# A cross-attention block in float32 on one core: the TensorE order goes from pairs of steps to fours

## What is computed

```python
x = layer_norm(hidden_states, ln1_w, ln1_b)
q = (x @ q_w + q_b)   # 8 x 256 x 256, split in 16 heads of 16
k = (encoder_hidden_states @ k_w + k_b)
v = (encoder_hidden_states @ v_w + v_b)
scores = jnp.einsum('bhqd,bhkd->bhqk', q, k) * scale
scores = jnp.where(mask, scores, mask_value)
attn = jax.nn.softmax(scores, axis=-1)
out = jnp.einsum('bhqk,bhkd->bhqd', attn, v)
out = out.transpose(0, 2, 1, 3).reshape(B, LQ, D) @ cproj_w + cproj_b
hidden = out + residual
y = layer_norm(hidden, ln2_w, ln2_b)
y = jax.nn.gelu(y @ fc_w + fc_b, approximate=True) @ proj_w + proj_b
return hidden + y
```

## Time and profile before

| | |
|---|---|
| median of 3 runs | 770.86 us (765.46 to 772.29) |
| profiled execution, device time | 768.76 us |
| its span (first to last instruction) | 767.0 us |
| TensorE (PE) busy | 702.5 us, 92% |
| ScalarE (ACT) busy | 446.1 us, 58% |
| VectorE (DVE) busy | 371.3 us, 48% |
| mean granted TensorE clock | 0.965 of full speed |

### The profile page before, as it was taken

How to read it: one execution, slowest core, us unless ns; L and a number is a source line. 1 busy time by engine, 2 the same in 40 slices (tenths; PEclk the granted TensorE clock), 3 DMA queues, 4 the chain that set the end, 5 groups by cost and what they waited for, 6 DMA issues and landing times.

```text
span 767.0 us, 16866 instructions
## 1 busy us (share of the span) xinstructions
PE 702.5 (92%) x7026; PEld 478.5 (62%) x7026; DVE 371.3 (48%) x824; ACT 446.1 (58%) x475; POOL 120.9 (16%) x90
## 2 busy tenths in 40 slices
PE   3657699899999999999999999999998978999997
PEld 3545466566656656666566566656664544597897
DVE  6643355265436534643464446534642331467663
ACT  3004366856676677567756775676566788733321
POOL 5222002200220032003201220131000600110010
PEclk9867799999999999999999999999999989999999
DMA  9787578657874788477938694878475800000000
GB/s 312 216 186 131 186 184 188 179 138 183 189 203 128 174 188 217 143 180 158 235 123 203 148 246 123 192 153 230 132 165 126 253 6 2 1 21 8 29 28 31
DMA packets 51275, 113.78 MB, mean 148 GB/s; under 512 B 7050, under 2 KB 40178, under 8 KB 49914
## 3 DMA queue, kind: packets, MB, share of 16 engines
q1 hardware_dynamic: 40700, 80.47, 44.5%
q10 hardware_dynamic: 10494, 32.17, 13.8%
HBM read 65.30 MB, written 47.06 MB: 146 GB/s over the span
## 4 chain that ended last, share of the span: by engine, by line
PE 76%; ACT 13%; DMA 5%; DVE 3%; issue 2%; ACTq 1%; DVEq 0%
PE O L1126 21%; PE S L1119 16%; ACT pr L583 11%; PE O L1056 10%; PE XB L1056 10%; PE O L1213 6%; PE S L1056 6%; DMA k_scr<-kpart 2%; DMA qst<-q_scr 2%; PE XB L1093 2%; PE XB L1153 2%; PE MB L1106 2%; DVE kpart L725 1%; DVE kpart L728 1%; DMA cols_s<-in_cols 1%
## 5 line engine op out<-in xcount | busy, mean ns | idle before, releaser
L583 ACT ACTIVATE pr<-S 128x1024 f32<-128x1024 f32 x416 | 400.6, 1024 | 188.6 <-PE S L1119 184.4
L1126 PE MATMUL O<-pr,vsl 128*17 128x256 f32 x3328 | 227.4, 388 | 1.3 <-DVE ot L790 1.3
L1119 PEld LDWEIGHTS S<-qst,kst 50*128 50x128 f32 x1664 | 117.1, 188 | 120.4 <-ACT pr L583 81.4
L1119 PE MATMUL S<-qst,kst 50*128 50x256 f32 x1664 | 171.7, 315 | 18.7 <-ACT pr L583 15.0
L1126 PEld LDWEIGHTS O<-pr,vsl 128*17 128x17 f32 x3328 | 75.3, 97 | 79.2 <-issue 17.7
L725 DVE TENSOR_SCALAR kpart<-O,cols_s 128x384 fp32r<-128x384 f32 x64 | 40.6, 635 | 120.7 <-PE O L1056 120.7
L771 DVE TENSOR_REDUCE mx<-MB 128x2 fp32r<-128x512 f32 x64 | 44.1, 690 | 79.0 <-PE MB L1106 79.0
L510 POOL CAST c_hi<-cT 128x768 fp32r<-128x768 f32 (+1 forms) x28 | 23.9, 852 | 348.0 <-DMA cT<-in_ctx_t 235.8
L1056 PE MATMUL XB<-w_hi,c_hi 128*128 128x256 f32 (+1 forms) x208 | 68.3, 328 | 2.1 <-DVE vsl L739 1.3
L739 DVE TENSOR_TENSOR vsl<-XB,rows_s 128x256 f32<-128x256 f32 (+1 forms) x104 | 43.3, 417 | 55.1 <-PE XB L1056 55.1
L1056 PE MATMUL O<-c_hi,w_hi 128*128 128x384 f32 (+1 forms) x128 | 52.6, 411 | 17.7 <-POOL c_lo L515 10.3
(11 more groups left out here) (100 smaller groups left out, 825.6 us busy)
## 6 DMA issues: line engine op xcount, KB each, us to landing
kst<-k_scr SPq DMA_DIRECT2D x59, 400.2 KB
k_scr<-kpart SPq DMA_DIRECT2D x48, 384.0 KB, 8.0
v_scr<-vsl ACTq DMA_DIRECT2D x8, 1768.0 KB, 11.9
kst<-k_scr SPq DMA_DIRECT2D x59, 200.1 KB
cT<-in_ctx_t ACTq DMA_DIRECT2D x21, 384.0 KB, 7.6
k_scr<-kpart SPq DMA_DIRECT2D x16, 449.0 KB, 7.1
q_scr<-qpart SPq DMA_DIRECT2D x16, 256.0 KB, 2.5
qst<-q_scr SPq DMA_DIRECT2D x59, 64.0 KB
```

The lines of the kernel that those rows point to most:

```text
L583: nc.scalar.activation(pr[:, n % PBUF, :], S[:, 2 * (n % 2):2 * (n % 2) + 2, :] .rearrange("p a n -> p (a n)"), ACT.Exp).then_inc(s_.exp_d ...
L1119: last = nc.tensor.matmul(S[:, 2 * (n % 2) + g_, j * LQ:(j + 1) * LQ], kst[rows_, s, j, kt * P:(kt + 1) * P], qst[rows_, s, j, :], start=T ...
L1126: last = nc.tensor.matmul(O[32 * h:32 * h + VW, 0, 0:LQ], vsl[:, par, s, kt, h * VW:(h + 1) * VW], pr[:, n % PBUF, h * LQ:(h + 1) * LQ], s ...
```

## The change

The tables now go by fours ("quads") of steps, 13 a batch. A four is: its max unit, the scores of two steps, its V, xt, q or cproj unit (`x_units`), its K unit, the scores of the other two steps, and then the value products of four steps, those numbered 4i-2 to 4i+1. One V unit now makes two key tiles (12 matmuls, one read-out of 512 columns), so there are 7 instead of 13. There is at most one K unit and one unit of `x_units` in a four: K units in fours 0, 1, 3, 4, 5, 7, 8 and 10, V units in 0, 5, 6, 9, 10, 11 and 12 (the last has one tile), cproj in 1, xt in 2, q in 3, max units in 1, 2, 5, 6, 8, 9, 11 and 12. In batch 7 only cproj, y's transposes (four 9) and the max units of fours 1, 2, 5 and 6 are left. STRADDLE is empty: where a slot ends inside a four (i = 3, after its third step; i = 10, after its first; i = 0 of the next batch, after its second), the next step's value products stand right behind, and wait for `o_taken`; VectorE has its read-outs of the four's units ahead of the `take_o`. The buffers `pr` go from 4 to 6, the encoder states and `vsl` change their layout, `max_evac` reads KB first, the head is put in another order, SyncE's list of stores and fills follows the new order, `store_v` always goes at n = 10, `load_mlp` moves from n = 44 of batch 6 to n = 4 of batch 7, and y's transposes of batch 7 go to n = 38. Numbers of matmuls, exponentials and transfers and their bytes stay.

The diff, cut to its core:

```diff
-PBUF = 4
+PBUF = 6
 STEPS = SLOTS * KT
-PAIRS = STEPS // 2
+QUADS = STEPS // 4
...
-K_AT = {0: (0, 0), 2: (0, 1), 4: (0, 2), 6: (0, 3), 8: (1, 0), 10: (1, 1), 12: (1, 2), 14: (1, 3)}
...
-CPROJ_AT, XT_AT, Q_AT = 3, 4, 5
...
-STRADDLE = (7, 20)
+K_AT = {0: (0, 0), 1: (0, 1), 3: (0, 2), 4: (0, 3), 5: (1, 0), 7: (1, 1), 8: (1, 2), 10: (1, 3)}
...
+CPROJ_AT, XT_AT, Q_AT = 1, 2, 3
+STRADDLE = {}
...
+KV = -(-KT // 2)
...
-        vsl = sb("vsl", [P, 2, SLOTS, KT, HG * VW], F32)
+        vsl = sb("vsl", [P, 2, KT, H * VW], F32)
...
                 first_fill(sp, b, 3)
                 if b + 1 < B:
-                    for c in range(3):
-                        store_k(b + 1, 0, c)
+                    store_k(b + 1, 0, 0)
+                    store_k(b + 1, 0, 1)
                 first_rows(b, 2)
                 if b + 1 < B:
+                    store_k(b + 1, 0, 2)
                     store_q(b + 1)
                     store_k(b + 1, 0, 3)
                     first_fill(sp, b + 1, 0)
                     store_k(b + 1, 1, 0)
-                    store_k(b + 1, 1, 1)
                 first_rows(b, 3)
                 if b + 1 < B:
+                    store_k(b + 1, 1, 1)
+                    first_fill(sp, b + 1, 1)
                     store_k(b + 1, 1, 2)
-                    first_fill(sp, b + 1, 1)
+                    first_rows(b + 1, 0)
                     store_k(b + 1, 1, 3)
-                    first_rows(b + 1, 0)
                     first_fill(sp, b + 1, 2)
                     first_rows(b + 1, 1)
...
             for b in range(B):
                 for n in range(STEPS):
-                    if n == 10 and b == 0:
-                        store_v(0)
+                    if n == 10:
+                        store_v(b)
                     if n in CTX_AT and b + 2 < B:
                         next_ctx(b + 2, CTX_AT.index(n))
-                    if n == 48 and b + 1 < B:
-                        store_v(b + 1)
-                    if n == 44 and b + 2 == B:
+                    if n == 4 and b + 1 == B:
                         load_mlp()
-                    if b == 0 and n == 40:
+                    if b == 0 and n == 46:
                         x_root(2 * QT, TOK, XB_VAR)
                     if b == B - 1 and n == 20:
                         h_root(first, 0, 0, HEAD)
-                    if b == B - 1 and n == 2 * YT_AT + 4:
+                    if b == B - 1 and n == 4 * YT_AT + 6:
                         act.wait_ge(mlpw_lo, 2)
                         y_t(first, 0)
-                    exponential(first, b, n)
+                    exponential(first, b, n, (STEPS * b + n) % PBUF)
...
-            def v_evac(b, kt):
-                m = TAIL if kt == KT - 1 else P
-                if kt == 0:
+            def v_evac(b, i):
+                tiles = slice(2 * i, min(2 * i + 2, KT))
+                m, n = (P, 2) if i < KV - 1 else (TAIL, 1)
+                if i == 0:
                     dve.wait_ge(pads_set, 7 if b == 0 else 10)
                     if b >= 2:
                         dve.wait_ge(v_out, 16 * (b - 1))
-                dve.wait_ge(xb_ready, v_use(b, kt) + 1)
+                dve.wait_ge(xb_ready, v_use(b, i) + 1)
                 nc.vector.tensor_tensor(
-                    vsl[0:m, b % 2, :, kt, :].rearrange("p s (h w) -> p s h w", w=VW)[:, :, :, 0:HD],
-                    XB[0:m, 0:D].rearrange("p (s h d) -> p s h d", s=SLOTS, d=HD),
-                    bv_s[0:m, :].rearrange("p (s h d) -> p s h d", s=SLOTS, d=HD), ALU.add).then_inc(xb_taken, 1)
+                    vsl[0:m, b % 2, tiles, :].rearrange("p t (h w) -> p t h w", w=VW)[:, :, :, 0:HD],
+                    XB[0:m, 0:n * D].rearrange("p (t h d) -> p t h d", t=n, d=HD),
+                    bv_s[0:m, :].rearrange("p (h d) -> p h d", d=HD).unsqueeze(1).broadcast_to([m, n, H, HD]),
+                    ALU.add).then_inc(xb_taken, 1)
...
+                dve.wait_ge(kb_ready, kb + 1)
+                nc.vector.tensor_reduce(mx[:, s % 2, :, NJ + j], KB.rearrange("p (q k) -> p q k", q=QT), AX.X, ALU.max,
+                                        negate=True).then_inc(kb_taken, 1)
                 dve.wait_ge(mb_ready, mb + 1)
                 nc.vector.tensor_reduce(mx[:, s % 2, :, j], MB[:, :].rearrange("p (q k) -> p q k", q=QT), AX.X, ALU.max,
                                         negate=True).then_inc(mb_taken, 1)
-                dve.wait_ge(kb_ready, kb + 1)
-                nc.vector.tensor_reduce(mx[:, s % 2, :, NJ + j], KB.rearrange("p (q k) -> p q k", q=QT), AX.X, ALU.max,
-                                        negate=True).then_inc(kb_taken, 1)
                 if j == NJ - 1:
...
             k_evac(0, 0, 0)
-            head(0)
+            newton(rs_rows(rs1, 0, 2 * QT), ln_steps, XA_VAR, ln_root, 1)
             k_evac(0, 0, 1)
-            head(1)
-            newton(rs_rows(rs1, 0, 2 * QT), ln_steps, XA_VAR, ln_root, 1)
+            x_normalise(0)
+            v_evac(0, 0)
+            xt_evac(HEAD_X.index("xt"))
             k_evac(0, 0, 2)
-            head(2)
-            x_normalise(0)
+            q_evac(0, HEAD_X.index("q"))
             k_evac(0, 0, 3)
-            xt_evac(HEAD_X.index("xt"))
-            q_evac(0, HEAD_X.index("q"))
             for c in range(CH):
                 k_evac(0, 1, c)
-                head(3 + c)
-            head(7)
-            max_evac(0, 0, 0, len(HEAD_K), 0)
-            head(8)
-            max_evac(0, 0, 1, len(HEAD_K) + 1, 1)
-            head(9)
-            head(10)
-            max_evac(0, 1, 0, len(HEAD_K) + 2, 2)
-            head(11)
-            max_evac(0, 1, 1, len(HEAD_K) + 3, 3)
-            head(12)
-
-            def units(b, p):
+                v_evac(0, 1 + c)
+            max_evac(0, 0, 0, HEAD_K.index("m00"), HEAD_MAX.index("m00"))
+            v_evac(0, 5)
+            max_evac(0, 0, 1, HEAD_K.index("m01"), HEAD_MAX.index("m01"))
+            v_evac(0, 6)
+            max_evac(0, 1, 0, HEAD_K.index("m10"), HEAD_MAX.index("m10"))
+            max_evac(0, 1, 1, HEAD_K.index("m11"), HEAD_MAX.index("m11"))
...
+                for i in range(QUADS):
+                    if i in MAX_AT and b + MAX_AT[i][0] < B:
+                        d, s, j = MAX_AT[i]
+                        max_evac(b + d, s, j, kb_use_max(b, i), mb_use(b, i))
+                    if i not in STRADDLE:
+                        x_units(b, i)
+                    if i in K_AT and b + 1 < B:
+                        k_evac(b + 1, *K_AT[i])
+                    if i == 0 and b > 0:
+                        take_o(b - 1, 3)
+                    if i == 3:
                         take_o(b, 0)
-                    if p == 20:
+                    if i == 6:
+                        take_o(b, 1)
+                    if i == 10:
                         take_o(b, 2)
-                    units(b, p)
-                    if p == 13:
-                        take_o(b, 1)
-                    if p == 0 and b > 0:
-                        take_o(b - 1, 3)
-                    norms(b, p)
+                    if i in STRADDLE:
+                        x_units(b, i)
+                    if i == 0 and b > 0:
+                        divide(b - 1, 3)
+                    if i == 3:
+                        divide(b, 0)
+                    if i == 6:
+                        divide(b, 1)
+                    if i == 10:
+                        divide(b, 2)
+                    norms(b, i)
...
-            def v_unit(b, kt):
-                c, m = CHUNK[kt], TAIL if kt == KT - 1 else P
-                cut = slice((kt - T0[c]) * P, (kt - T0[c]) * P + m)
-                pe.wait_ge(lo_done, CH * b + c + 1)
-                bank_free(xb_taken, v_use(b, kt))
-                product3(XB[0:m, 0:D], [(c_hi[:, c, k, cut], c_lo[:, c, k, cut]) for k in range(KC)],
-                         [(w_hi[:, 1, k, :], w_lo[:, 1, k, :]) for k in range(KC)]).then_inc(xb_ready, 1)
...
+            def v_unit(b, i):
+                bank_free(xb_taken, v_use(b, i))
+                for t, kt in enumerate(range(2 * i, min(2 * i + 2, KT))):
+                    c, m = CHUNK[kt], TAIL if kt == KT - 1 else P
+                    cut = slice(kt * P, kt * P + m)
+                    pe.wait_ge(lo_done, CH * b + c + 1)
+                    last = product3(XB[0:m, t * D:(t + 1) * D], [(c_hi[:, k, cut], c_lo[:, k, cut]) for k in range(KC)],
+                                    [(w_hi[:, 1, k, :], w_lo[:, 1, k, :]) for k in range(KC)])
+                last.then_inc(xb_ready, 1)
...
-                for p in range(PAIRS):
-                    for n in (2 * p, 2 * p + 1):
-                        scores(b, n)
-                    before = [(b, n - 2) if n >= 2 else (b - 1, STEPS + n - 2) for n in (2 * p, 2 * p + 1)]
-                    if p in STRADDLE:
-                        values(*before[0])
-                        units(b, p)
-                        values(*before[1])
-                    else:
```

(24 more changed lines are left out.)

237 lines of the change are left out of this document (108 added, 129 removed).

## The result

| | before | after |
|---|---|---|
| time, median of 4 runs | 769.91 us (765.46 to 772.29) | 828.81 us (824.0 to 831.47) |
| ratio, with its 95% interval | 1 | 1.0765 (1.069 to 1.0841) |
| the profiled execution, its span | 768.76, 767.0 | 831.47, 829.7 |
| mean granted clock of TensorE | 0.965 | 0.929 |
| TensorE's waits for a fill, whole span | 16.2 us | 57.0 us |

The change costs 7.7%. 777 us (764 to 790) was forecast, so the time lies far outside the range.

A forecast was written before the change was run, and what follows sets the result against it. TensorE's order was taken to bound batches 0 to 6, with the exponentials nearly the bound in batch 7. Terms 0 - 1.9 + 2.9 + 7.4 = +8.4 on 768.76 us gave 777, range 764 to 790.

The forecast's parts named there:

- prices of blocks: TensorE's cost per block, start to start: 1.85 us for four steps' value products, 0.66 for two steps' scores.
- I take 0, so batches 0 to 6 stay as they are: Net per batch 0 to 6: -1.95 - 1.35 + 0.4 + 3.15 = +0.25 us, taken as 0.
- slot ends are bare: Three slot ends a batch without a covering unit cost 0.87 us each plus 0.55: 3.15 us lost per batch.
- stall for `load_mlp`: TensorE's idle of 1.82 us in batch 6 vanishes with the load moved to batch 7: 1.9 us saved.
- rival 3: Slower by a late fill of slot 0: 2 us late in 7 batches gives 791 us; chance 0.2.
- 14 remain: Time left from issue of slot 0's fill, some 32 us into the batch, to its max unit at 46.5.
- own sign: Idle of TensorE before max units outside batch 0 would show that slot 0's fill comes late.
- so the fill takes 9 to 15: Slot 0's fill, issue to landing, in us, read from when transfers went quiet in the earlier trace.
- Rival 4: Unit groups cost more (786 us) or TensorE's clock falls (one or two more stretches in batch 7: 780 to 782); chance 0.18.
- 7.4 lost: Batch 7: 0.85 us for each of nine fours without units, plus smaller terms; bounds 2 and 10.
- 2.9 lost: Batch 0's first max unit of slot 2 waits for the fill with 3.4 us of work behind, less 0.5.
- what the fours give, the bare slot ends take: In batches 0 to 6 savings of 1.95 and 1.35 us a batch are offset by 3.15 lost at slot ends.

The follow-up runs named there:

- e13: Changed kernel with K units earlier (fours 0 to 5, 7, 8), max units of slots 2 and 0 one four later, batch 7 in twos; 755.23 us, ratio 0.9837.
- e8: Changed kernel without the second `kst` transfer in each half of a fill from batch 1 on; 783.68 us, ratio 1.0209.
- e10: e8 with batch 7's steps in twos, as before the change; 762.49 us, ratio 0.993.
- e9: e8 with a unit put back at the slot ends in fours 0, 3 and 10; 773.56 us, ratio 1.009.
- e1: Changed kernel with a unit put back at the slot ends in fours 0, 3 and 10; 834.58 us, ratio 1.0809.
- e6: Changed kernel, max units of slots 2 and 0 one four later, three K units one four earlier, slot ends in fours 0, 3, 10 covered; 801.88 us, ratio 1.047.
- e15: e13 with the units of fours 0 and 3 moved from the four's middle into the slot end; 774.78 us, ratio 1.0094.
- e7: Changed kernel, max units of slots 2 and 0 one four later, three K units one four earlier, batch 7's value products in pairs; 777.01 us, ratio 1.0114.

## Why the prediction was wrong, step by step

**The steps that held.** The prices of blocks came as forecast: four steps' value products take 1.85 (250.48 plus 1.85 is the next block's start in e13), a unit's group costs the same between scores as before. The sum for batches 0 to 6, "I take 0, so batches 0 to 6 stay as they are", holds once no fill is late: e8's period is 73.7 against 74.30, and e13's is 72.7 to 74.1 in batches 2 to 6. The slot ends are bare as read from the earlier trace rows. In the timeline of after, in four 10 of batch 4, the second block starts 472.25 - 470.92 = 1.33 after the first instead of 0.43, so 0.90 is lost:

```profile
470.92 0.63 PE L1130 MATMUL O<-pr,vsl 128*17 128x256 f32 x8
472.25 1.49 PE L1130 MATMUL O<-pr,vsl 128*17 128x256 f32 x24 [0.70 <-DVE ot L791]
```

The bare slot ends are 23 and not the 24 that were counted, as none falls into four 0 of batch 0; they cost TensorE 11.9 us of named waits in 16 places and 5.0 in 7 more that the trace puts down to issue. The stall for `load_mlp` is gone, as said.

**The step that failed: the fill's landing time, and with it rival 3's weighing.** The sum put waits for fills in batches 0 to 6 at nothing, and rival 3 priced them: "If the fill comes 2 us late, 7 x 2 = 14: 791." They are 33.7 us. The place, the mechanism and the sign of this rival were right, and so was the time left: "14 remain", and 12.5 to 14.4 was measured. The prediction's own sign came too, idle time of TensorE before max units outside batch 0. Wrong was "so the fill takes 9 to 15". I had read the landing from the earlier trace rows, as the moment after which the DMA share was low. The fills in question took 14.2 to 22.1 us. Two things were left out. The new place sets the fill of slot 0 beside three loads of encoder states, the first 2 us behind it, where before there were two, and the next slot's fill follows 12.9 us behind it instead of 15.7; the DMA share in 190 to 200 is 1.04 at 172 GB/s. How much of the landing time is due to these neighbours no run tells; the one fill without the loads landed soonest, and e8 shows only that a fill with fewer bytes is in time. And the same reasoning was not made for slot 2's fill, which gave 12.0 of the 33.7 us. The Trainium skill has the rule in "DMA: Bandwidth & Descriptors", section "Issuing engines are not separate DMA queues": transfers started by different engines interleave on the same 16 DMA engines. The trace agrees as far as it goes: ScalarE's loads and SyncE's fill stand in one stretch in which the DMA share is 1.04.

The bound to use was plain in the same rows. Before, the reader came 21.7 us after the issue, and that was all that was shown to be enough; 14 was shown by nothing. With 21.7 as the upper end of the need the rival reads 7 x (21.7 - 13.8) = 55 us, which the range to 790 does not hold.

**The second step: what a wait does to the clock.** Rival 4 gave the half clock one or two stretches more in batch 7. It comes behind seven of the thirteen waits for a fill, and in fours with no unit. A max unit, scores, K unit and scores behind such a wait take 216.19 - 211.12 = 5.07, where the same blocks at full clock, behind the wait of 2.10 us in batch 3, take 381.19 - 377.84 = 3.35. Beside the 33.7 us of waits, 50.7 - 33.7 = 17.0 us more were lost up to batch 7. Part of that is batch 7's own fours, which start before slot 0's end, so the two can't be parted exactly from this sum. Two runs part them otherwise: e8, with no late fill, is 45 us under the changed kernel, and e10, with batch 7 in twos as well, another 21, which together is the whole loss and a little more; both move fewer bytes than the kernel before, so this is a division of the loss and not a fair race with it. The Trainium skill says it in "TensorE: Matmul & The Clock Gate", section "HAM oscillation — how this bites in real kernels": waits for a transfer in each round of a loop let the engine throttle, and the next round starts cold. The trace agrees for seven of the thirteen waits, with 2.21 us for a K unit of 1.25 behind one; behind five the clock stays full. The direction of rival 4 was right. Its "the full clock in batches with such short waits speaks" against half clock holds for the bare slot ends of batches 0 to 6 (e8, 1.00 from 100 to 590), and fails for the fours of batch 7, in which waits for exponentials stand close together (e8, 0.75 from 620 to 680).

**Batch 7: right in mechanism, too small.** "7.4 lost". e10 against e8 gives 21.2 with nothing else different. The fours without a unit were priced at full clock (4.81), and 0.87 for a slot end; in e8 a four with both takes 664.20 - 656.81 = 7.39 instead of 5.68.

**The head: wrong.** "2.9 lost" was nothing: slot 0 of batch 0 ends at 99.50 against 99.48. The max unit's wait did end sooner (80.91 against 82.88), by 2.0 instead of the 0.5 taken, and only 2.0 us more of work lay behind it (99.50 - 80.91 against 99.48 - 82.88), instead of 3.4.

**What remained open.** That "what the fours give, the bare slot ends take" is near in size (e9: 10.1 us for 20 slot ends, 0.5 each net, against the 0.87), but the remedy wasn't had in any of the kernels with all transfers: e1, e6 and e15 all got slower or stayed. For e6 the traces point to an emptied middle, though no run sets that apart; for e15 the cause is open.

## What to carry to other kernels

Where a reorder moves the producer of a transfer back or its reader forward, take as proven only the time that the old schedule gave it, here 21.7 us, and not the stretch in which the transfers look busy; then ask what else will share the transfers in the new place. Count a new wait of some microseconds on TensorE with the half clock behind it, and give every group of steps some unit in its middle (e13 against e7). A loss that stays when one suspect is removed may be moved: look where the next wait went before the suspect is cleared, and before a good idea is dropped, since the same fours with the units at other places are 1.6% faster than the kernel before.

## What the runs showed of the hardware

- A wait of 2.26 us on TensorE was followed by half clock up to 459.04, 3.7 us on, and one of 2.10 us by none; a wait of 8.27 us had its clock at 0.55 already from 206 to 210, at 0.50 from 210 to 214 and at 0.67 from 214 to 218, when TensorE worked again.
- Short waits that came close together did the same in batch 7 of e8: behind 0.89 and 0.41 us the records are at half clock from 659.78 on, and the clock from 620 to 680 is 0.75. Behind a like pair 10 us earlier they are at full clock. Bare slot ends of 0.7 to 0.8 us amid full work left no such trace: 20 of them, from 100 to 590 in e8, at a clock of 1.00.
- The same fill of ten transfers landed 14.2 to 22.1 us after its issue in one kernel, soonest where no load of encoder states ran beside it. A DMA share of 1.04 went with 172 GB/s (190 to 200) and, right behind, with 281 (200 to 206), and one of 0.80 with 177 GB/s in the kernel before (326 to 341): the GB/s alone don't tell how busy the DMA engines are.
